# Layer norm split over two engines and GELU over two items in a local attention network on one Trainium2 core

## What is computed

```python
x = shift_tokens(x)                       # in front of the attention
q, k, v = split(x @ Wqkv)                 # 16 heads of 64
q, k = rotary(l2norm(q)), rotary(l2norm(k))
out = local_attention(q, k, v)            # windows of 32 keys and the 32 before
x = out @ Wo + residual
mu = x.mean(-1, keepdims=True); var = ((x - mu) ** 2).mean(-1, keepdims=True)
xn = (x - mu) / jnp.sqrt(var + 1e-05) * g + bln
hg = xn @ W1 + b1                         # 128 -> 2 * 341
a, gate = jnp.split(hg, 2, -1)
x = a * gelu(gate) @ W2 + b2 + residual
```

## Time and profile before

| what | us |
|---|---|
| median of three runs (5441.48 to 5457.64) | 5452.23 |
| the profiled execution's own time | 5452.7 |
| its span, first to last instruction | 5450.9 |
| TensorE busy (matmuls) in the span | 5026.2 (92%) |
| VectorE busy | 4764.0 (87%) |
| ScalarE busy | 4045.7 (74%) |
| GpSimd busy | 3152.2 (58%) |
| of the 2900 us from 1000 to 3900: TensorE, VectorE, ScalarE, GpSimd busy | 2774.6, 2684.4, 2340.1, 1951.1 |

### The profile page before, as it was taken

One profiled execution on the slowest core, in us unless ns is written; L12 is line 12 of the kernel. 1 busy time (PEld: TensorE's weight loads), 2 busy tenths in 40 slices (PEclk: granted clock), 3 DMA queues, 4 the chain that ended last, 5 costly groups with the idle time before them and its releaser, 6 DMA issues. The chain is left out here.

```text
span 5450.9 us, 109430 instructions
## 1 busy us (share of the span) xinstructions
PE 5026.2 (92%) x34408; PEld 3517.0 (65%) x34408; DVE 4764.0 (87%) x8649; ACT 4045.7 (74%) x11685; POOL 3152.2 (58%) x2280
## 2 busy tenths in 40 slices
PE   6997899999999999999999999999999999688887
PEld 4664667767667676666767666676667777444543
DVE  4666899999899998999989999899999999398897
ACT  2554688888788887888778888788888788577764
POOL 0001766666666666666666666666666666144444
PEclk9998999999999999999999999999999999788887
DMA  1000000000000000000000000000000000000000
GB/s 22 6 5 20 7 1 1 0 6 15 2 0 0 6 15 2 0 1 4 17 2 0 1 1 21 2 0 1 0 14 3 0 1 0 5 3 3 3 3 5
DMA packets 35461, 26.80 MB, mean 5 GB/s; under 512 B 11203, under 2 KB 29190, under 8 KB 35078
## 3 DMA queue, kind: packets, MB, share of 16 engines
q1 hardware_dynamic: 26302, 22.22, 1.4%
q10 hardware_dynamic: 8776, 0.45, 0.1%
HBM read 20.56 MB, written 2.10 MB: 4 GB/s over the span
## 5 line engine op out<-in xcount | busy, mean ns | idle before, releaser
L1246 POOL TENSOR_TENSOR b_w<-b_w,b_vt 128x512 f32<-128x512 f32 x768 | 981.5, 1278 | 1292.6 <-DVE b_vt L1155 659.0
L1250 POOL TENSOR_TENSOR b_rn<-b_ssm,all_neg_half 128x16 f32<-128x16 f32 x384 | 1127.6, 2936 | 32.0
L1072 ACT ACTIVATE b_PT<-ps 128x512 f32<-128x512 f32 x768 | 463.7, 604 | 432.8 <-PE ps L927 411.1
L1054 ACT ACTIVATE b_Pr<-ps,b_nm 128x128 f32<-128x128 f32 x1536 | 565.8, 368 | 209.8 <-DVE b_nm L1181 207.9
L1181 DVE TENSOR_REDUCE b_nm<-ps 128x4 f32<-128x640 f32 x768 | 630.7, 821 | 103.3 <-PE ps L907 94.4
L975 PE MATMUL ps<-b_Whi,b_xlo 128*128 128x512 f32 x1152 | 586.0, 509 | 40.8 <-DVE b_vt L1155 24.5
L1056 ACT ACTIVATE b_Pr<-ps,b_nm 128x160 f32<-128x160 f32 x1536 | 611.9, 398 | 0.0
L1153 DVE TENSOR_TENSOR b_w<-ps,until_b_rotab 128x512 f32<-128x512 f32 x768 | 529.2, 689 | 55.0 <-ACT b_sq L1087 40.2
L1087 ACT ACTIVATE b_sq<-ps 128x512 f32<-128x512 f32 x768 | 469.2, 611 | 82.7 <-PE ps L977 82.1
L1155 DVE TENSOR_TENSOR b_vt<-ps,until_b_rotab 128x512 f32<-128x512 f32 x768 | 522.9, 681 | 0.0
L1157 DVE TENSOR_REDUCE b_ss<-b_sq 128x8 f32<-128x512 f32 x768 | 519.4, 676 | 0.0
(11 more groups left out here) (269 smaller groups left out, 12585.9 us busy)
## 6 DMA issues: line engine op xcount, KB each, us to landing
b_Wraw<-in_L_ffn_Wqkv SPq DMA_DIRECT2D x36, 256.0 KB, 2.8
b_Wo<-in_L_ffn_Wo SPq DMA_DIRECT2D x6, 512.0 KB, 4.7
a_xtok<-in_L_attn_hidden_states SPq DMA_DIRECT2D x16, 128.0 KB, 2.1
out<-c_xout SPq DMA_DIRECT2D x16, 128.0 KB, 1.8
b_W<-in_L_ffn_W SPq DMA_DIRECT2D x6, 341.0 KB, 3.0
setup_wmod<-in_L_wmod SPq DMA_DIRECT2D x2, 384.0 KB
b_W<-in_L_ffn_W SPq DMA_DIRECT2D x6, 128.0 KB
setup_rot<-in_rot SPq DMA_DIRECT2D x1, 256.0 KB
```

The lines of the kernel that those rows point to most:

```text
L1054: nc.scalar.activation(s.Pr[:, p % 2, j, 0:P], ps[:, S_BANK[j], WIN:KEYS], ACT.Exp, bias=s.nm[:, h, 0:1], accum_out=s.ssum[:, h, 0:1])
L1246: nc.gpsimd.tensor_tensor(rows, rows, s.vt[:, i % 4], ALU.add).then_inc(s.pool_add, 1)
L1250: nc.gpsimd.tensor_tensor(s.rn[:, j], s.ssm[:, j], g.neg_half[:, 0:HB], ALU.pow).then_inc(s.pool_r, 1)
```

## The change

It does two things, in the attention phase alone.

**Layer norm.** `centred_stats` takes mean and variance straight out of the bank, and then subtracts the mean out of the bank into `b_xtok` in one instruction of 256 columns; the copy falls away. The bank is given free by the subtraction. GpSimd, behind its power, multiplies the centred rows by it (`scaled_pool`). VectorE's slot 14 has no layer norm any more. The copy of the two parameter columns moves to the start of the step, with a buffer for each parity.

**GELU.** `b_hgate` and `b_ha` have a half for each parity. Odd steps run one GELU over both halves, 1536 columns, in slot 11; even steps run none. For that the gate product, W2 and the last residual of an item come one step later than before: they are a stage of their own (`closing`, item n - 3), in the same slots. There is one more step at the end, and in step 2 a use of the bank without a reader (`vacant`), which keeps the two banks' turns alike.

The core of the diff:

```diff
+def centred_stats(nc, dve, ln, src, free, n):
...
+    nc.vector.tensor_tensor(ln.var[:], ln.mv[:, :, 1], ln.var[:], ALU.add).then_inc(ln.var_ready, 1)
+    nc.vector.tensor_tensor(ln.xn[:], src, ln.mv[:, :, 0:1].broadcast_to((P, TT, P)), ALU.subtract).then_inc(free, 1)
+def scaled_pool(nc, pool, ln, g, free, uses, n):
+    pool.wait_ge(ln.var_ready, n + 1)
+    nc.gpsimd.tensor_tensor(ln.rstd[:], ln.var[:], g.neg_half[:, 0:TT], ALU.pow).then_inc(ln.rstd_ready, 1)
+    pool.wait_ge(ln.rstd_ready, n + 1)
+    pool.wait_ge(free, uses)
+    nc.gpsimd.tensor_tensor(ln.xn[:], ln.xn[:], ln.rstd[:].rearrange("p (t o) -> p t o", o=1).broadcast_to((P, TT, P)), ALU.mult).then_inc(ln.normed, 1)
...
-    for n in range(ITEMS - 1, ITEMS + 2):
+    for n in range(ITEMS - 1, ITEMS + 3):
         whole(n)
...
+                    if slot == W2_SLOT and (step.closing is not None or step.vacant):
+                        bank = take_spare(("w2", 0))
...
+                            pe.wait_ge(s.hg_ready, u)
...
-                    if step.ffn is not None and slot == GELU_SLOT:
+                    if step.ffn is not None and step.odd and slot == GELU_SLOT:
                         b, uses = step.spare(("w1", 2))
                         act.wait_ge(s.spare_free[b], uses + 1)
-                        nc.scalar.activation(s.hgate[:], s.hgate[:], ACT.Gelu).then_inc(s.gelu_done, 1)
+                        nc.scalar.activation(s.hgate[:], s.hgate[:], ACT.Gelu).then_inc(s.gelu_done, 2)
...
-                    if step.tail is not None and slot == NORMED_SLOT:
-                        layernorm_apply(nc, dve, s.ff, s.xtok, t)
-                        nc.vector.tensor_scalar_mul(s.lnp[:], g.lparam[:, bass.ds(lt, 1), 0:2].rearrange("p a k -> p (a k)"), 1.0).then_inc(s.lnp_ready, 1)
...
-                        nc.vector.tensor_copy(s.xtok[:], ps[:, SPARE[b], 0:NT].rearrange("p (t e) -> p t e", t=TT)).then_inc(s.spare_free[b], 1)
-                        dve.wait_ge(s.spare_free[b], uses + 1)
-                        layernorm_stats(nc, dve, s.ff, s.xtok, t)
+                        centred_stats(nc, dve, s.ff, ps[:, SPARE[b], 0:NT].rearrange("p (t e) -> p t e", t=TT), s.spare_free[b], t)
...
-                    if step.ffn is not None and slot == GATE_SLOT:
-                        pool.wait_ge(s.gelu_done, u + 1)
-                        nc.gpsimd.tensor_tensor(s.ha[:], s.ha[:], s.hgate[:], ALU.mult).then_inc(s.hg_ready, 1)
+                    if step.closing is not None and slot == GATE_SLOT:
+                        pool.wait_ge(s.gelu_done, u + 1 if step.odd else u)
+                        nc.gpsimd.tensor_tensor(s.ha[:, 1 - step.odd], s.ha[:, 1 - step.odd], s.hgate[:, 1 - step.odd], ALU.mult).then_inc(s.hg_ready, 1)
```

More of the change, by code:

```diff
@@ L263, in layernorm_stats @@
     nc.vector.tensor_tensor(ln.var[:], ln.mv[:, :, 1], ln.var[:], ALU.add).then_inc(ln.var_ready, 1)
+def centred_stats(nc, dve, ln, src, free, n):
+    for tt in range(TT):
+        last = nc.vector.bn_stats(ln.st[:, tt], src[:, tt])
+    last.then_inc(ln.moment, 1)
+    dve.wait_ge(ln.moment, 2 * n + 1)
+    nc.vector.memset(ln.var[:], LN_EPS)
+    for tt in range(TT):
+        last = nc.vector.bn_aggr(ln.mv[:, tt], ln.st[:, tt])
+    last.then_inc(ln.moment, 1)
+    dve.wait_ge(ln.moment, 2 * n + 2)
+    nc.vector.tensor_tensor(ln.var[:], ln.mv[:, :, 1], ln.var[:], ALU.add).then_inc(ln.var_ready, 1)
[6 more added lines that the diff above has]
+    nc.gpsimd.tensor_tensor(ln.xn[:], ln.xn[:], ln.rstd[:].rearrange("p (t o) -> p t o", o=1).broadcast_to((P, TT, P)), ALU.mult).then_inc(ln.normed, 1)
 def layernorm_pool(nc, pool, ln, g, n):
@@ L703, in spare_uses @@
             uses += [("w1", W1_SLOT[slot])] if slot in W1_SLOT else []
-            uses += [("w2", 0)] if slot == W2_SLOT else []
+        if closing and slot == W2_SLOT:
+            uses.append(("w2", 0))
         if front and slot in TRANSPOSE_SLOT:
@@ L746, in whole @@
         stages = stages_of(n)
-        items = [divmod(n + d, NB) if there else None for d, there in zip((1, 0, -1, -2), stages)]
-        body(Step(n, n % 2, items[0], items[2], items[3], convert=n == -1))
+        items = [divmod(n + d, NB) if there and n + d >= 0 else None for d, there in zip((1, 0, -1, -2, -3), stages)]
+        body(Step(n, n % 2, items[0], items[2], items[3], items[4], convert=n == -1))
     def inner(l):
@@ L951, in body @@
                             give_spare(("w1", c), last)
-                        if slot == W2_SLOT:
-                            bank = take_spare(("w2", 0))
-                            pe.wait_ge(s.w2_in, 32 * lu + 32)
-                            pe.wait_ge(s.hg_ready, u + 1)
-                            for c, (_, width) in enumerate(FF_CHUNKS):
-                                last = nc.tensor.matmul(bank[:, 0:NT], s.W2[0:width, c], s.ha[0:width, c], start=c == 0, stop=c == 2)
-                            give_spare(("w2", 0), last)
+                    if slot == W2_SLOT and (step.closing is not None or step.vacant):
+                        bank = take_spare(("w2", 0))
+                        if step.vacant:
+                            pe.wait_ge(s.w2_in, 32)
+                        else:
+                            pe.wait_ge(s.w2_in, 32 * step.closing[0] + 32)
+                            pe.wait_ge(s.hg_ready, u)
+                        for c, (_, width) in enumerate(FF_CHUNKS):
+                            last = nc.tensor.matmul(bank[:, 0:NT], s.W2[0:width, c], s.ha[0:width, 1 - pa, c], start=c == 0, stop=c == 2)
+                        give_spare(("w2", 0), last)
                     if step.front is not None and slot in TRANSPOSE_SLOT:
@@ L1136, in body @@
                     x_lower, x_upper, x_all = g.xT[lower, bass.ds(dst, NT)], g.xT[upper, bass.ds(dst, NT - 1)], g.xT[:, bass.ds(dst, NT)]
+                    nc.vector.tensor_scalar_mul(s.lnp[:, step.odd], g.lparam[:, bass.ds(lt, 1), 0:2].rearrange("p a k -> p (a k)"), 1.0).then_inc(s.lnp_ready, 1)
+                if step.closing is not None:
+                    lw, end = known(step.closing[0]), known(step.closing[1] * NT)
+                    x_end = g.xT[:, bass.ds(end, NT)]
+                    kept = nc.vector.tensor_scalar_mul(s.lend[:], g.lparam[:, bass.ds(lw, 1), 2:3].rearrange("p a k -> p (a k)"), 1.0)
+                    if step.ffn is None:
+                        kept.then_inc(s.lp_ready, 1)
                 if step.ffn is not None:
[L1138 to L1139 removed]
+                    lu = known(step.ffn[0])
                     nc.vector.tensor_scalar_mul(s.lp[:], g.lparam[:, bass.ds(lu, 1), 2:9].rearrange("p a k -> p (a k)"), 1.0).then_inc(s.lp_ready, 1)
@@ L1220, in body @@
                         rotate(slot - 1)
-                    if step.ffn is not None and slot == END_SLOT:
+                    if slot == END_SLOT and (step.closing is not None or step.vacant):
                         b, uses = step.spare(("w2", 0))
                         full_spare(("w2", 0))
-                        nc.vector.scalar_tensor_tensor(out=x_end, in0=ps[:, SPARE[b], 0:NT], scalar=s.lp[:, 0:1], in1=x_end,
-                                                       op0=ALU.add, op1=ALU.add).then_inc(s.spare_free[b], 1)
-                        dve.wait_ge(s.spare_free[b], uses + 1)
-                        dve.sem_inc(s.x_ready, 1)
+                        if step.vacant:
+                            dve.sem_inc(s.spare_free[b], 1)
+                        else:
+                            dve.wait_ge(s.lp_ready, u + 1)
+                            nc.vector.scalar_tensor_tensor(out=x_end, in0=ps[:, SPARE[b], 0:NT], scalar=s.lend[:], in1=x_end,
+                                                           op0=ALU.add, op1=ALU.add).then_inc(s.spare_free[b], 1)
+                            dve.wait_ge(s.spare_free[b], uses + 1)
+                            dve.sem_inc(s.x_ready, 1)
             split_input(0, 0, 0)
```

45 lines of the change are left out of this document (22 added, 23 removed).

## The result

The changed kernel took 5462.09 us in the median of 20 runs (5452.95 to 5476.97), the kernel before 5453.27 us in 20 runs beside it: ratio 1.0019, interval 1.0012 to 1.0026. It is slower by some 9 us where 11 us less were forecast. That is inside the range of 5400 to 5490 and within the 0.3% that was called no change, but the sign is wrong, by more than the runs are uncertain.

A forecast was written before the change was run, and what follows sets the result against it. TensorE was taken to wait for VectorE's chain of slots 8 to 12 and ScalarE's chain up to slot 12's exponentials. 48 x (-0.86 + 0.58) + 2 = -11 us from 5452.2 gave 5441 us, range 5400 to 5490.

The forecast's parts named there:

- a gain in slot 9: VectorE's copy out of the bank becomes a subtraction with one semaphore wait less: 0.15 us gained, bounds 0 to 0.2.
- W2's wait: Even steps: TensorE's W2 product finds GpSimd's later gate product just ended; 0.1 us charged.
- the edges: One step added at the end of the phase: 2 us in all, bounds 0 and 5.
- GELU's columns: Odd steps, ScalarE: 768 more columns in GELU cost 0.72 us and move the scores of slot 14.
- theory B: Set up for the experiments: steps exchange a net gain as forecast; the loss comes from edges, later stage or lock.
- The forecast case: Whole kernel: even steps gain 0.86 us, odd lose 0.58, 11 us less in all; chance 0.61, bounds 5425 to 5458.
- 0.67 + 0.14: Even steps: TensorE's lost time before the scores of slot 14 and before the next step's opening scores, both gained.
- The 0.14: Odd steps: TensorE's loss before the next step's opening scores is given back, as the last exponentials no longer await VectorE.
- rival 2: Odd steps: the longer GELU costs nothing; 46 us less, 5407 us, or 5361 if odd steps gain too; chance 0.17.
- The first rival: Step's start: the moved copies wait for GpSimd's power; 56 us slower, 5508 us, or 5490 if partly absorbed; chance 0.12.

The follow-up runs named there:

- Run 5: The changed kernel with the gate product of even steps in GpSimd's slot 5 instead of 11: 5437.12 us, ratio 0.9962 to the kernel before.
- run 8: The changed kernel with odd steps' GELU over 768 columns instead of 1536, the even items' GELU left out: 5434.49 us, ratio 0.9958 to the kernel before.
- run 7: The changed kernel, but GELU of 768 columns in slot 3 of every step, gate product in slot 11: 5399.88 us, ratio 0.9900 to the kernel before.
- run 9: run 4 with one VectorE sum of squares moved from slot 11 behind the two products of slot 12: 5316.28 us, ratio 0.9748 to the kernel before.
- run 3: The changed kernel with the layer norm as before, so the GELU part alone: 5478.9 us, ratio 1.0036 to the kernel before.
- run 4: The changed kernel, but GELU of the closing item alone in slot 3 of every step, gate product in slot 5: 5373.91 us, ratio 0.9848 to the kernel before.

## Why the prediction was wrong, step by step

The sum failed in five terms: a gain in slot 9 that did not come, a loop turn that was not in it, W2's wait and the edges taken too small, and GELU's columns taken too large. In us of the kernel they are 48 x 0.15 = 7.2, 30 x 0.17 = 5.1, 48 x 0.11 = 5.3, 2.2 and -48 x 0.09 = -4.3, together 15.5 of the 16.5 between the forecast -11.4 and the profile's +5.1. 4.2 of these 5.1 are edges, as theory B had it; the steps alone come out even. The forecast case's own bounds, 5425 to 5458, leave the result out (with the bounds named for the terms the lower one comes to 5431); the wider range held it by room that was left for rivals that did not occur.

- **The form was right.** The steps alternate (41.7 and 43.1 were forecast, 42.05 and 43.23 came), table loads halved, VectorE's freed time became a wait for scores, W2's product waited for GpSimd. The net of two terms near 0.8 and 0.6 us is small, so small errors decided its sign: forecast -0.28 us a pair, measured +0.02.
- **Even steps, 0.67 + 0.14:** both came in full; the scores follow at 0.24 us in slot 14 and in the next slot 0.
- **Even steps, "I take 0.15 us" for slot 9: it was nothing.** VectorE began the next product 24.42 instead of 24.59 us into the step and then stood 0.18 us before the maximum of slot 10 (2224.02, above), where TensorE is not late. The chain that I followed back from slot 12 starts at those scores; I had traced it back to slot 8 only because the kernel before shows no idle time in between.
- **W2's product, "I charge 0.1 us": it was 0.21.** The product was put at 0.7 us as work; with the wait for GpSimd's own power it is 0.8, and the gate product had no slack left for it. The prediction's own numbers gave more than it charged: a W2 product moved 0.9 us up starts at 2015.76, and the gate product ends at 2016.0. Run 5 gave 0.18 back.
- **The loop turn was missing: 0.17 us a pair.** In a loop, ScalarE's first copy of an odd step starts late by about 1 us. Before, TensorE reached that place so late that this cost 0.12 us a pair (85.25 against 85.13); after, 0.29 (85.29 against 85.00). The trace of before had it: inside the loops the copy into `b_PT` starts some 1.4 us into odd steps and 0.58 into even ones. The rows that I read are the end of step 33 and the start of step 34, neither with a turn of the inner loop in front of it, and I had taken every step for alike.
- **Odd steps, 0.72 for 768 columns: 0.63.** GELU went from 0.85 to 1.49 us. That error alone was in the change's favour. The 0.14 came back as forecast. ScalarE is back to back from GELU to the exponentials, so rival 2, the longer GELU for nothing, is out; run 8 shows the price directly.
- **Edges, 2 us: 4.2**, within the bounds of 0 and 5: 2.7 at the end, and 1.5 at the start, where the doubled buffers are filled first, which I had not counted.
- **The first rival is refuted.** With the long power in flight (2238.61, 2.93 us) the moved copies took 0.16 and 0.15 us (2239.26, 2239.32). Of the 96 copies into `b_lnp` 91 ran wholly inside a power, and none of the 96 exceeded 0.17. By the port rule that I cited from the Trainium skill (SBUF — State Buffer, "Who interferes with whom") they would have waited; the measurement decides against it for this power. For GpSimd's sums the rule agrees with the rows: one took 2.28 us beside VectorE's product, and the old copy 1.25 beside a sum.

Summed by these terms a pair comes to -0.67 - 0.14 + 0.21 + 0.63 - 0.15 + 0.17 = +0.05, measured +0.02. With the edges the measured pair gives 48 x 0.02 + 4.2 = 5.2 us in the profile, which shows 5.1; the runs show 9 (7 to 14 by the interval). What remains, a few us, is of the size by which the unchanged phases and the steps behind a turn of the outer loop vary from profile to profile, and stays open.

## What to carry to other kernels

When a change takes time from one kind of step and gives it to another, compute each kind to its next bound separately, and ask for the idle place on the same engine before asking for fewer instructions: GELU with two table loads in slot 3 of every step (run 7) was 1.2% better than one pair in slot 11 of every second step (the result). Before crediting an engine with a shorter block, look for the next wait that it will run into; a gain ahead of such a wait is nothing, and a reduction that nobody reads yet can be moved out of a chain for the whole distance to the next start (0.59 us in run 9). Read a step of each parity and one outside the loop; their difference was a term that this sum lacked.

## What the runs showed of the hardware

- A loop turn has a price that depends on the slack around it: ScalarE's first copy behind a turn came 1.14 us later (2.71 against 1.57). The pair of steps paid 0.03 us in run 3, where TensorE's opening scores are 0.31 us late for another reason, 0.12 before the change, where they are 0.14 late, and 0.21 to 0.40 in the other kernels with two steps a body, where they are not late.
- A longer loop body can cost more than the turns it saves: with two steps a body one queue of instruction loads is silent inside the loops (1.98 MB in all) and another brings five packets of 8 KB a pair; with four steps the first carries 4.98 MB, and a turn costs 5.7 us in the mean.
- The lock between VectorE and GpSimd is not the same in both directions for the power. With a power in flight copies took 0.16 us and the product of 128x1024 its 1.23. In run 4 a power that began 0.04 us behind the start of such a product took 3.97 us instead of 2.93, and the 92 powers of that run that began inside one took 3.84 to 4.01:

```profile
2205.70 1.23 DVE L1198 TENSOR_TENSOR b_w<-b_w,b_rn 128x1024 f32<-128x1024 f32 x1
```
```profile
2205.74 3.97 POOL L1283 TENSOR_TENSOR b_rn<-b_ssm,all_neg_half 128x16 f32<-128x16 f32 x1
```
